# A context fetch in two DMAs of 112 and 13 rows, issued after a batch's K writes in a four-layer attention kernel

## The reference

```
K = (ctx_n @ kw + kb); V = (ctx_n @ vw + vb)          # 1500 keys for each of 16 batches
attn = softmax(Q K^T / sqrt(8));  out = attn @ V       # for each of 16 heads
x = x + out @ ow + ob
```

## Time and profile before

| | |
|---|---|
| Median of 3 runs | 1983.4 us (1973.65 to 1998.68) |
| Span of the profiled execution, first to last instruction | 1981.9 us |
| Mean granted TensorE clock | 0.873 of full speed |
| Busy: PE / PE weight load / DVE / ACT / POOL | 83% / 53% / 58% / 51% / 34% |
| DMA moved | 166.33 MB, mean 84 GB/s |
| Context fetches in `cx` | 56 (48 of them in layers 1 to 3), and 8 more in the ring of layer 0, 750 KB each |

### The profile page before, as it was taken

The page is one execution under the profiler, slowest core; times in us unless marked ns, Lnnn a source line. Parts: engine busy times, 40 slices in busy tenths (PEclk is TensorE's granted clock), DMA queues, the critical chain, the costliest instruction groups (busy, mean ns, idle before and its releaser), DMA issues.

```text
span 1981.9 us, 54153 instructions
## 1 busy us (share of the span) xinstructions
PE 1648.7 (83%) x20495; PEld 1047.8 (53%) x20495; DVE 1151.3 (58%) x2289; ACT 1006.1 (51%) x1911; POOL 676.4 (34%) x899
## 2 busy tenths in 40 slices
PE   4788787698988997785898998987883988999986
PEld 3465544365665665342465666654441566666654
DVE  5454444566676674454766776762453766667652
ACT  1243322166676675232466776762331566667662
POOL 7000055055565543236355666410241112222210
PEclk9898989599898997786798999997895789899987
DMA  5021103233443431005444444420005334444310
GB/s 180 30 74 68 47 23 86 57 97 108 119 117 111 117 103 56 1 1 115 99 112 114 119 118 117 111 85 1 1 6 138 83 112 116 118 118 119 104 47 10
DMA packets 178538, 166.33 MB, mean 84 GB/s; under 512 B 67551, under 2 KB 168098, under 8 KB 178402
## 3 DMA queue, kind: packets, MB, share of 16 engines
q1 hardware_dynamic: 176818, 163.35, 29.9%
q10 hardware_dynamic: 1008, 1.05, 0.2%
q0 software_dynamic: 576, 0.02, 0.0%
HBM read 114.46 MB, written 40.08 MB: 78 GB/s over the span
## 4 chain that ended last, share of the span: by engine, by line
PE 44%; DMA 16%; SPq 10%; issue 9%; DVE 9%; ACT 6%; POOL 6%; DVEq 0%; POOLq 0%; ACTq 0%
DMA k_dram<-k_lo 12%; SPq L420 7%; PE PS L1149 6%; PE PS L885 5%; PE PS L1175 4%; PE PS L1044 4%; POOL cx L602 4%; PE PS L1038 4%; DMA k_st<-k_dram 3%; PE PS L1123 3%; PE PS L964 3%; PE PS L1033 3%; DVE mx L1547 2%; PE PS L1249 2%; PE PS L982 2%
## 5 line engine op out<-in xcount | busy, mean ns | idle before, releaser
L1547 DVE TENSOR_REDUCE mx<-PS 112x1 f32<-112x500 f32 x1152 | 716.8, 671 | 325.7 <-PE PS L1123 322.4
L818 ACT ACTIVATE q_parts<-PS 125x448 f32<-125x448 f32 x1152 | 561.8, 543 | 109.1 <-PE PS L1175 104.8
L1123 PE MATMUL PS<-k_st,q_mx 50*112 50x500 f16 x1152 | 270.4, 416 | 93.7 <-DMA k_st<-k_dram 42.1
L567 POOL CAST k_hi<-k_full 128x500 f16<-128x500 f32 x144 | 87.4, 607 | 698.0 <-ACT k_full L748 352.3
L602 POOL TENSOR_SCALAR cx<-cx,norm_b 125x128 f32<-125x128 f32 x384 | 304.9, 808 | 60.0 <-DMA cx<-in_ctx 37.3
L1175 PEld LDWEIGHTS PS<-q_st,k_st 50*125 50x125 f16 x4608 | 190.6, 143 | 216.3 <-ACT q_parts L818 151.9
L1175 PE MATMUL PS<-q_st,k_st 50*125 50x112 f16 x4608 | 268.3, 239 | 39.4 <-ACT q_parts L818 23.2
L1149 PE MATMUL PS<-q_parts,v_sb 125*18 125x112 f32 x9216 | 296.8, 273 | 0.0
L1149 PEld LDWEIGHTS PS<-q_parts,v_sb 125*18 125x18 f32 x9216 | 222.4, 102 | 54.2 <-issue 44.5
L569 POOL TENSOR_TENSOR k_lo<-k_full,k_hi 128x500 f16<-128x500 f32 x144 | 163.9, 1138 | 21.1 <-POOL k_hi L567 4.5
L1123 PEld LDWEIGHTS PS<-k_st,q_mx 50*112 50x112 f16 x1152 | 99.5, 137 | 135.3 <-issue 99.8
(11 more groups left out here) (267 smaller groups left out, 2098.4 us busy)
## 6 DMA issues: line engine op xcount, KB each, us to landing
k_st<-k_dram SPq DMA_DIRECT2D x864, 62.5 KB, 2.2
cx<-in_ctx SPq DMA_DIRECT2D x56, 750.0 KB
k_dram<-k_hi SPq DMA_DIRECT2D x144, 125.0 KB, 1.8
k_dram<-k_lo SPq DMA_DIRECT2D x144, 125.0 KB, 1.9
v_sb<-in_ctx SPq DMA_DIRECT2D x8, 750.0 KB
q_mx<-q_all SPq DMA_DIRECT2D x48, 99.8 KB
q_st<-q_all SPq DMA_DIRECT2D x48, 99.8 KB
q_all<-q_dram SPq DMA_DIRECT2D x18, 196.0 KB, 6.4
```

Source lines behind the costliest of these rows:

```text
L818: act.activation(probs[:, c % RING, u * HR:(u + 1) * HR], PS[0:KC, (2 * c + u) % SC_RING, 0:HR], ACT.Exp).then_inc(sem("exp_done"), 1)
L1123: mm(PS[0:PW, MX_BANK + u % MX_RING, 0:TK], q_mx[64 * a:64 * a + ROWS, p, k, :], k_st[64 * a:64 * a + ROWS, p, k, TK * t:TK * t + TK], sta ...
L1547: dve.tensor_reduce(mx[:, r, t:t + 1], PS[0:PW, MX_BANK + u % MX_RING, 0:TK], AX.X, ALU.max)\
```

## The change

The fetch of a batch's context is issued as two DMAs, partitions 0 to 111 and 112 to 124, both counting on the same semaphore, so every wait for a fetch asks for 32 per batch instead of 16. This holds for all 64 fetches. In `attend` the fetch moves from its place ahead of `k_out(behind, 0)` to the place behind `k_out(behind, 2)`.

```
+CX_ROWS = ((0, 112), (112, KC))
+LOADED = 16 * len(CX_ROWS)
...
+                def fetch(dst, b, signal):
+
+                    rows = ctx[bass.ds(b, 1)].rearrange("o (p c) d -> (o p) c d", p=KC)
+                    for lo, hi in CX_ROWS:
+                        sp.dma_start(dst[lo:hi], rows[lo:hi]).then_inc(sem(signal), 16)
...
-                    sp.dma_start(cx[:, p, :, :], ctx[bass.ds(b, 1)].rearrange("o (p c) d -> (o p) c d", p=KC))\
-                      .then_inc(sem(f"cx_loaded{p}"), 16)
+                    fetch(cx[:, p, :, :], b, f"cx_loaded{p}")
...
-                    sp.dma_start(cx0[r], ctx[bass.ds(b, 1)].rearrange("o (p c) d -> (o p) c d", p=KC))\
-                      .then_inc(sem(f"cx0_loaded{r}"), 16)
+                    fetch(cx0[r], b, f"cx0_loaded{r}")
...
                     if behind:
                         q_max(behind)
-                        if not (isinstance(b, int) and b + 4 >= B):
-                            load((b + 4, i + 2, p))
                         k_out(behind, 0)
                         k_in(behind, 0)
                         k_out(behind, 1)
                         k_in(behind, 1)
                         k_out(behind, 2)
+                        if not (isinstance(b, int) and b + 4 >= B):
+                            load((b + 4, i + 2, p))
...
-                    ge_known(pool, (f"cx_loaded{p}", 16 * (B // 2 * (layer - 1) + i + 1)),
+                    ge_known(pool, (f"cx_loaded{p}", LOADED * (B // 2 * (layer - 1) + i + 1)),
```

More of the change, by code:

```diff
@@ L951, in turn_ctx @@
                 if t == 0:
-                    pe.wait_ge(sem(f"cx0_loaded{r}"), 16 * (i + 1))
+                    pe.wait_ge(sem(f"cx0_loaded{r}"), LOADED * (i + 1))
                 ge(pe, "cxT0_done", NT * b + t)
@@ L1028, in misc @@
                             if cr["norm"] is None:
-                                pe.wait_ge(sem(f"cx_loaded{p}"), 16 * (B // 2 * cr["n"] + i + 1))
+                                pe.wait_ge(sem(f"cx_loaded{p}"), LOADED * (B // 2 * cr["n"] + i + 1))
                             else:
@@ L1405, in row_stats @@
                 b, i, p, r = batch
-                dve.wait_ge(sem(f"cx0_loaded{r}"), 16 * (i + 1))
+                dve.wait_ge(sem(f"cx0_loaded{r}"), LOADED * (i + 1))
                 for c in range(C):
```

## The result

The changed kernel takes 2065.73 us (median of 4 runs, 2053.24 to 2073.74), the one before 1981.49 us (4 runs). Ratio 1.04, 95% interval 1.0357 to 1.0443. The forecast was 2010 us in a range of 1970 to 2055, so its median lies 11 us above the range and 56 us above the forecast. The profiled execution has a span of 2071.9 us against 1981.9 before. Two runs further down, 1913.18 us of the split alone (the one that its trace shows) and 2534.59 us of the move alone, fell into a slower state of the chip and are left out of the medians and ratios.

The account below looks back on a forecast made before the run. The prediction took SP's loop of transfers, with the fetch blocking the first K write, as the bound. Layer 3 at -28, layer 2 at +31 and layer 1 at +23 gave +26, so 2010 us, range 1970 to 2055.

Parts of the forecast that it names:

- the 6.3 us jam at the first write: In SP's queue, the first K write stands behind the context fetch, which costs SP's loop 6.3 us each time.
- Layer 3: Cross stage where a later fetch hurts nobody: PE becomes the bound, 340 against 368.3 us, -28 us.
- SP's own loop: SP's queue, q_st to q_st: falls from 24.6 to 18.7 us, so SP alone bounds nothing above 22 us.
- The POOL loop in layers 1 and 2: Fetch, POOL's normalising and splitting, K writes, next fetch: a new loop of 27.4 us per batch, 11 turns.
- Rival 1: The fetch-to-fetch loop through POOL doesn't bind, PE bounds everywhere: -84, 1900 us; chance 0.12.
- I take 4.5 us: Landing time of the split context fetch, between bounds of 4.4 and 8.5 us; first term of the 27.4 us loop.
- Rival 2: The fetch lands later than 4.5 us behind the third K write, deciding from 5.1; at 6.4, 2052 us; chance 0.20.
- Layer 1: Cross stage where the fetch-to-fetch loop through POOL binds: end at 787.7 against 764.3, +23 us.
- layer 2: Cross stage where the fetch-to-fetch loop through POOL binds: end at 1354.4 against 1323.0, +31 us.
- The stall on k_st: PE's first maximum in each attend of layers 1 and 2 waits some 4 us for a late stacking.
- POOL's wait: POOL's wait for `cx` in layers 1 and 2 rises from 1.8 to about 12 us per batch.

## Why the prediction was wrong in size and right in mechanism

- *What bounds before, the 6.3 us jam at the first write*: right. The split alone frees it and gives 92 us (1980.88 to 1888.88).
- *Layer 3*, -28 forecast: -31.1 measured. PE bounds it, steady attends of 22.1 and 23.1 us.
- *SP's own loop no longer binds*: right. In layer 2 of the changed kernel SP waited 156.1 us for POOL's k_lo and 43.9 for K writes.
- *The POOL loop in layers 1 and 2*: right as a mechanism, shown by taking its work away (1889), by lengthening it (2150) and by opening it (1895 with the fetch behind the first write, 1889 with the split alone). Rival 1, that it doesn't bind, is out.
- *The step that failed* is the first term of the sum, "I take 4.5 us" for the landing. It is 6.65. The runs price the 2.15: alone on the DMA engines 5.3 to 5.6, so about 1 from the bytes taking 3.0 us where I had 1.9 (5 engines' rate per engine was carried to 16, with no start and end); about 0.66 from the third write ahead of it; the rest from the stackings beside it. Rival 2 had named the place behind the third write, from 5.1 us up, and gave it 0.20; that covers the second half of the 2.15 but not the first, which a fetch with nothing beside it shows too. Its price of 2.2 us for each 0.1 us makes 2.15 into +47.
- *The remaining part*: on the spans the forecast was 2008 and the measurement 2071.9, +64. Layer 1 is 41 over its forecast, layer 2 30, layer 3 -3, the rest -4. Landing accounts for 11 turns x 2.15 = 24 in each of the two. Of the other 17 in layer 1, 11 are longer turns: they average 30.63 us from the fetch of batch 4 to that of batch 15, and layer 2's 29.64. Most of that lies between the K writes (5.8 and 5.6 us a step in the mean, where layer 2 has 5.2 and 5.5), with slow issuing by SP such as in these rows; two of PE's unexplained 5 us waits fall into layer 1 as well. In the run that waits for the third write, which has none of them, layers 1 and 2 are equally long, 434 us each. The forecast had neither in its sum. The last 6 us in each of the two layers stay unassigned.

```profile
503.75 2.42 SPq L414 DMA_DIRECT2D k_dram<-k_lo  x1
...
545.53 4.11 SPq L426 DMA_DIRECT2D k_st<-k_dram  x6
```

- *The stall on k_st*, 4 us forecast: 3.82 in the attend shown, 4.0 in the mean of layer 2's 12. *POOL's wait*, 12 us forecast: 14 to 15, longer as the landing is.
- *The Trainium skill*, DMA: Bandwidth & Descriptors, Rules for kernel authors, advises against two transfers to disjoint partition halves. Here the split took 3.0 us off a lone landing and 4.5% off the kernel at the old place, so the measurement decides against it. The same page's section on why a DMA increments its semaphore by 16 has a rule for the number of engines (5 for 125 rows, 16 for 112), and the runs bear it out: a DMA share of 0.31 for 125 rows, and up to 381 GB/s in the lone split fetch, where five engines moved 128. The share itself, 0.93 to 1.11 there, is too rough to count the engines by. What I did not weigh: this gain is 3.0 and not the 4.1 of going from 6.0 to 1.9 us.

What stays open: how the last 1.1 us of landing divide between the stackings and the write ahead, since single fetches scatter by 0.5 to 0.7 us; why SP's issuing is slow in some turns of layer 1; and what PE's 5 us waits there are.

## What to carry to other kernels

When a transfer is moved behind another queue's step, follow it to its reader and from there back to the issue: if the reader's next task feeds the step that it was moved behind, a loop has closed, and its period counts once per turn, whatever the engines' busy shares. Price a loop's terms as if each 0.1 us were multiplied by its turns, above all a landing that no row shows: take apart the time before the first byte, the bytes, and the time after the last one, and measure it once alone. And try the parts of a change one by one, since here the split alone gains 4.5% and the combined change loses 4%. A place for a transfer that closes no loop can be two steps away: the same split fetch behind the first K write instead of the third gives 1895 us instead of 2066.

## What the runs showed of the hardware

- A DMA of 125 rows of 6 KB runs at a share of 0.31 of 16 engines and lands after 8.3 us alone; the same rows as 112 + 13 land after 5.3 us, 3.0 of them with bytes moving, up to 381 GB/s.
- What is issued just behind a 125-row fetch is held up at either place tried: the first K write is stacked after 8.6 us, or the second after 8.3 us, instead of 2.3. Behind a split fetch it was 2.7 us for a write issued 4.1 us later, and 4.5 for the second write issued 4.0 us later with six stackings between.
- The unsplit fetch lands after 10.3 us behind the third K write and beside the stackings, 2.0 more than alone; the split one after 6.5, 1.0 more than alone (means of layer 2's turns).
- In layer 3, attends without a stall held the granted clock at 0.99 over 337 us.
- In layer 1, PE idled 4.8 to 5.4 us ahead of a group of scores with nothing in the profile that ended it, none to two times in the traces of the kernels that PE bounds; each went with 9 to 10 us more for the layer.
